# Swapping the operands of a one-hot sort product, splitting its address steps into two bfloat16 halves, and counting with the first matching steps

## The reference

```python
xn = layernorm(x)
agg = segment_sum(xn[dst] * edge_weight[:, None], src)     # rows gathered per edge, summed per source node
gnn = relu((xn + agg) @ W1 + b1) @ W2 + b2
x2 = x + gnn + head_mix(xn)                # 8 heads, k'v over all nodes, then q @ kv, plus xn
y  = x2n + sum over the top 2 of 16 experts of weight * expert(x2n)   # x2n = layernorm(x2)
out = x2 + layernorm(y) * gamma + beta
```

## Time and profile before

| | us |
|---|---|
| median of 3 runs | 2087.97 |
| lowest, highest | 2083.77, 2088.9 |
| the profiled execution, its own time | 2086.33 |
| its span | 2084.2 |
| TensorE matmul busy | 1814.0 |
| VectorE busy | 1411.1 |
| ScalarE busy | 741.2 |
| GpSimd busy | 1206.1 |

### The profile page before, as it was taken

How to read it: one execution, slowest core, us unless ns; L and a number is a source line. 1 busy time by engine, 2 the same in 40 slices (tenths; PEclk the granted TensorE clock), 3 DMA queues, 4 the chain that set the end, 5 groups by cost and what they waited for, 6 DMA issues and landing times. The chain is left out here.

```text
span 2084.2 us, 43884 instructions
## 1 busy us (share of the span) xinstructions
PE 1814.0 (87%) x12300; PEld 1634.0 (78%) x12300; DVE 1411.1 (68%) x4015; ACT 741.2 (36%) x2167; POOL 1206.1 (58%) x1244
## 2 busy tenths in 40 slices
PE   6306999758889999999999999999977999999986
PEld 4206889657878888888888888878766999999974
DVE  5899788758996777677767776657554555555547
ACT  5806778500101333333333332222222333333347
POOL 1003444477777777777777777777703555555424
PEclk9657999979999999999999999999978999999999
DMA  5000101054444444444444444444425642222248
GB/s 174 0 0 21 39 22 39 22 166 149 137 132 120 129 127 129 130 134 129 128 129 128 130 125 125 123 121 128 120 84 163 208 126 72 72 72 72 69 148 316
DMA packets 130018, 232.33 MB, mean 111 GB/s; under 512 B 25990, under 2 KB 82616, under 8 KB 129703
## 3 DMA queue, kind: packets, MB, share of 16 engines
q0 software_dynamic: 56096, 144.39, 23.8%
q1 hardware_dynamic: 46039, 59.76, 8.8%
q10 hardware_dynamic: 27696, 25.83, 3.9%
HBM read 187.46 MB, written 42.43 MB: 110 GB/s over the span
## 5 line engine op out<-in xcount | busy, mean ns | idle before, releaser
L1337 POOL DMA_INDIRECT lower<-xn_rows,lower x858 | 826.9, 964 | 261.5 <-issue 232.8
L1502 DVE TENSOR_SCALAR lower<-bank,lower 128x128 f32<-128x128 f32 x960 | 347.1, 404 | 69.6 <-issue 53.1
L1362 PE MATMUL bank<-ones,ident 128*128 128x128 f32 x2376 | 322.5, 278 | 23.3 <-DVE xh L1519 17.8
L1362 PEld LDWEIGHTS bank<-ones,ident 128*128 128x128 f32 x2376 | 307.4, 192 | 40.4 <-DVE xh L1519 20.7
L1378 PE MATMUL bank<-lower 128*128 x960 | 292.2, 386 | 19.9 <-SPq L1207 13.1
L1519 DVE TENSOR_TENSOR xh<-xh,bank 128x256 f32 x480 | 199.3, 415 | 158.4 <-PE bank L1379 156.9
L1379 PE MATMUL bank<-lower 128*128 x960 | 287.3, 380 | 0.0
L608 POOL DMA_INDIRECT edge_records_sorted<-lower x112 | 113.2, 1011 | 292.3 <-ACT lower L771 266.7
L2003 DVE TENSOR_SCALAR arena<-bank,b_tile 128x128 f32<-128x128 f32 x456 | 128.4, 345 | 166.4 <-PE bank L1881 166.4
L1881 PEld LDWEIGHTS bank<-arena 128*128 128x128 f32 x1824 | 224.6, 194 | 14.6 <-ACT arena L1936 8.9
L1881 PE MATMUL bank<-arena 128*128 128x128 f32 x1824 | 225.6, 278 | 8.1 <-ACT arena L1936 8.1
(11 more groups left out here) (347 smaller groups left out, 2594.7 us busy)
## 6 DMA issues: line engine op xcount, KB each, us to landing
lower<-xn_rows,lower POOLq DMA_INDIRECT x858
lower<-in_L_ffn_w SPq DMA_DIRECT2D x16, 512.0 KB
upper<-in_L_ffn_w SPq DMA_DIRECT2D x16, 512.0 KB
xn_rows<-xh SPq DMA_DIRECT2D x7, 896.0 KB, 4.1
lower<-xn_rows ACTq DMA_DIRECT2D x49, 128.0 KB
xn_rows<-lower ACTq DMA_DIRECT2D x49, 128.0 KB
x_plus_beta<-lower ACTq DMA_DIRECT2D x49, 128.0 KB
upper<-in_x SPq DMA_DIRECT2D x1, 6144.0 KB
```

What stands on the lines that cost most here:

```text
L1337: pool.indirect_dma_start(edge_rows[:, t % ROUND, :], None, xn_dram, bass.IndirectOffsetOnAxis(source.bitcast(U32)[:, t:t + 1], 0)).then_i ...
L1362: pe.matmul(sums_at(u)[:, 0:P], ident[:], ones[:], start=True, stop=True)
L1502: dve.tensor_scalar(edge_sel[:, (2 * u + h) % ESEL, :], iota_gather, lane[:, at:at + 1], weight_s[:, at:at + 1], ALU.is_equal, ALU.mult).t ...
```

## The change

The sort product takes `row_hot` as the stationary operand and `moving` as the moving one; its sums go from PSUM to `quads` in one ScalarE copy, and the transpose, `quads_across` and two semaphores are gone. The mask `past_m` is a bfloat16 matrix of zeros and ones, and the steps no longer multiply it on DVE: they are the moving operand `steps_b`, one column for a group, with the step's multiple of 128 on partitions 0 to 49 and its rest on partitions 64 to 113, both exact in bfloat16. DVE makes these in nine small operations before the first group. The counts stand behind distances 1 to 7. The ranks go to bank 3; a slot's `turn` waits until they have been read, instead of `second`, and `ranks` waits for the copy of the turn before it.

```diff
-        past_m = [carve(NQ * P)]
-        steps_col = carve(2 * NGRP)
+        past_m = [carve(NQ * P // 2).bitcast(BF16) for _ in range(2)]
+        LOW = 64
+        KB = LOW + NT + 1
+        first_col, step_col = carve(NGRP), carve(NGRP)
+        step_i, low_step = carve(NGRP).bitcast(I32), carve(NGRP).bitcast(I32)
+        steps_b = carve(NGRP // 2).bitcast(BF16)
...
-                if d % 4 == 3:
-                    count(d // 4)
+                if d <= NR:
+                    count(d - 1)
...
                 for c in range(NQ):
-                    mm = pe.matmul(bank[2 + p][:, c:c + 1], past_m[p][0:NT + 1, c * P:(c + 1) * P], ones[0:NT + 1, 0:1],
+                    mm = pe.matmul(bank[2 + p][:, c:c + 1], past_m[p][0:KB, c * P:(c + 1) * P], steps_b[0:KB, ds(g, 1)],
                                    start=True, stop=True)
...
                 if looped(r) or r >= 1 or i >= 2:
-                    pe.wait_ge(s_qx, g - 1)
+                    pe.wait_ge(s_qcp, g - 1)
                 for e in range(GC):
-                    mm = pe.matmul(bank[6 + p][0:NQ * QW, 0:P], moving[p][:, e].rearrange("p c w -> p (c w)"),
-                                   row_hot[p][:, e, :], start=e == 0, stop=e == GC - 1)
+                    mm = pe.matmul(bank[6 + p][:, 0:NQ * QW], row_hot[p][:, e, :], moving[p][:, e].rearrange("p c w -> p (c w)"),
+                                   start=e == 0, stop=e == GC - 1)
                 mm.then_inc(s_qmm, 1)
-                pe.wait_ge(s_qx, g + 1)
-                pe.sem_inc(s_apart, 1)
-                pe.transpose(bank[1][:, p * P:p * P + NQ * QW], quads_across,
-                             ident[0:NQ * QW, 0:NQ * QW]).then_inc(s_qT, 1)
...
                 act.wait_ge(s_qmm, 2 * g + 2)
-                act.activation(quads_across, bank[6 + p][0:NQ * QW, 0:P], ACT.Copy).then_inc(s_qx, 1)
-                act.wait_ge(s_qT, g + 1)
...
-                act.activation(quads[i], bank[1][:, p * P:p * P + NQ * QW], ACT.Copy).then_inc(s_qcp, 1)
+                act.activation(quads[i], bank[6 + p][:, 0:NQ * QW], ACT.Copy).then_inc(s_qcp, 1)
...
-            dve.tensor_copy(steps_col[0:NT + 1, :], bank[0][0:NT + 1, 0:2 * NGRP]).then_inc(s_dve, 1)
+            dve.memset(first_col, 0.0).then_inc(s_dve, 1)
+            dve.memset(steps_b, 0.0).then_inc(s_dve, 1)
+            dve.tensor_copy(step_col[high, :], bank[0][high, NGRP:2 * NGRP]).then_inc(s_dve, 1)
+            dve.tensor_copy(step_i[high, :], bank[0][high, NGRP:2 * NGRP]).then_inc(s_dve, 1)
+            dve.wait_ge(s_dve, n.add(5 + NQ))
+            dve.tensor_copy(first_col[high, :], bank[0][high, 0:NGRP]).then_inc(s_dve, 1)
+            dve.tensor_copy(first_col[low, :], bank[0][high, 0:NGRP]).then_inc(s_dve, 1)
+            dve.tensor_scalar(low_step[high, :], step_i[high, :], P - 1, None, ALU.bitwise_and).then_inc(s_dve, 1)
+            dve.wait_ge(s_dve, n.add(3))
+            dve.tensor_tensor(steps_b[high, :], step_col[high, :], low_step[high, :], ALU.subtract).then_inc(s_dve, 1)
+            dve.tensor_copy(steps_b[low, :], low_step[high, :]).then_inc(s_dve, 1)
...
-                dve.tensor_scalar(past_m[p][0:NT + 1, :], quad_number[0:NT + 1, :], steps_col[0:NT + 1, ds(g, 1)],
-                                  steps_col[0:NT + 1, ds(g + NGRP, 1)], ALU.is_ge, ALU.mult).then_inc(s_mov, 1)
+                dve.tensor_scalar(past_m[p][0:KB, :], quad_number[0:KB, :], first_col[0:KB, ds(g, 1)], None,
+                                  ALU.is_ge).then_inc(s_mov, 1)
...
-            while any(u + d - T_SECOND in turn_unit for d in (-1, 0, 1)):
+            while u in turn_unit or u - 1 in turn_unit:
                 u += 1
...
-        gate_at, ranks_at = bank[6][:, D:D + NX], bank[5][:, D:D + NX]
+        gate_at, ranks_at = bank[6][:, D:D + NX], bank[3][:, 0:NX]
```

More of the change, by code:

```diff
@@ L192, in gps_layer @@
         group_wgt = [carve(GC) for _ in range(2)]
-        past_m = [carve(NQ * P)]
-        steps_col = carve(2 * NGRP)
+        past_m = [carve(NQ * P // 2).bitcast(BF16) for _ in range(2)]
[4 more added lines that the diff above has]
+        steps_b = carve(NGRP // 2).bitcast(BF16)
         quad_idx = [carve(NQ).bitcast(U32) for _ in range(4)]
         quads = [carve(NQ * QW) for _ in range(4)]
-        quads_across = carve(P)[0:NQ * QW, :]
         aside = carve(NGRP)
@@ L316, in gps_layer @@
         past_all = xn_rows[:, 0:NJ * (NX - 1)]
-        past_m.append(xn_rows[:, 2 * F:2 * F + NQ * P])
-        assert 2 * F + NQ * P <= GT * D
         assert NJ * (NX - 1) <= GT * D
@@ L495, in gps_layer @@
         s_qmm = sem("quads_summed")
-        s_qx = sem("quads_across_copied")
-        s_qT = sem("quads_transposed")
         s_qcp = sem("quads_copied")
@@ L665, in edges_tensor @@
                     differences(d + 2)
-                if d % 4 == 3:
-                    count(d // 4)
-            assert GC // 4 == NR
+                if d <= NR:
+                    count(d - 1)
+            assert GC > NR
             pe.wait_ge(s_clear, 4)
@@ L936, in edges_vector @@
             dve.wait_ge(s_pref, 2 * len(BANKS) + 2 * NGRP)
-            dve.tensor_copy(steps_col[0:NT + 1, :], bank[0][0:NT + 1, 0:2 * NGRP]).then_inc(s_dve, 1)
-            dve.wait_ge(s_dve, n.add(2 + NQ))
+            high, low = slice(0, NT + 1), slice(LOW, KB)
+            dve.memset(first_col, 0.0).then_inc(s_dve, 1)
[9 more added lines that the diff above has]
+            dve.tensor_copy(steps_b[low, :], low_step[high, :]).then_inc(s_dve, 1)
+            dve.wait_ge(s_dve, n.add(2))
             def addresses(r, i):
@@ L1161, in gps_layer @@
         assert all(turn_unit[s] + T_CHOOSE < rank_unit[s] and turn_unit[s] + 4 <= turn_unit[s + 1] for s in range(NT - 1))
-        seconds_before = lambda u: sum(a + T_SECOND < u for a in turn_unit)
+        turns_before = lambda u: sum(a < u for a in turn_unit)
         ranks_before = lambda u: sum(a < u for a in rank_unit)
@@ L1400, in ranks @@
                         pe.wait_ge(s_hsum, s)
-                    pe.wait_ge(s_x2, seconds_before(rank_unit[s]))
+                    pe.wait_ge(s_hTe, turns_before(rank_unit[s]))
                     pe.matmul(ranks_at, ones_pb, hot_sum, start=True, stop=False)
@@ L1405, in turn @@
                 def turn(s):
+                    if ranks_before(turn_unit[s]):
+                        pe.wait_ge(s_place, ranks_before(turn_unit[s]))
                     pe.wait_ge(s_hin, s + 1)
@@ L1425, in second @@
                         pe.wait_ge(s_x2, s)
-                    if ranks_before(turn_unit[s] + T_SECOND):
-                        pe.wait_ge(s_place, ranks_before(turn_unit[s] + T_SECOND))
                     pe.matmul(bank[5][:, 0:D], ones[0:1, 0:P], gb2_row[0:1, :], start=True, stop=False)
```

## The result

The changed kernel takes 2197.7 us (median of 4 runs, 2195.8 to 2198.0), the kernel before 2088.4 beside it: a ratio of 1.0527, 95% interval 1.0508 to 1.0545, 109 us slower. The profiled execution took 2197.9 us, its span is 2195.9.

A forecast was written before the change was run, and what follows sets the result against it. TensorE's chain of product, copy, transpose and address products was taken to bound the sort. Sort stage +113.3, counts -1.0, steps +1.0, ranks 0 made +113 us, forecast 2200 us, range 2172 to 2212.

The forecast's parts named there:

- The clock: Edge sort: TensorE was taken to stay at 1.2 GHz for the whole stage with the swapped product.
- The first rival: Edge sort: 64-column streams keep TensorE at 2.4 GHz, period 6.6 us, -35 us, total 2053 us; chance 0.10.
- The sort's length: Edge sort: 28 periods of 12.46 us, last product ending at 519.4 us against 405.4, +114.0 us.
- The product: Edge sort on TensorE: 56 instructions at 214.5 ns each at 1.2 GHz, 12.0 us per product.
- the address products with the hand-over: Edge sort, each period: four bfloat16 address products 0.38 us, hand-over 0.07 us.
- the 0.4 us of each loop turn: Edge sort: each of six loop turns adds 0.4 us, as it had before the change.
- Product's end to first scatter: End of the sort: one copy of 0.25 us left, 1.1 us instead of 1.8, -0.7 us.
- Counts: Matching steps: counts behind steps 1 to 7 let the prefix products start at about 53.1 us, -1.0 us.
- Steps in two halves: Before the first sort group: nine small DVE operations replace one 0.20 us copy, +1.0 us (0.5 to 1.5).
- Ranks: Gather stage: moved ranks and new waits cost 0, bounds -0.5 and +1 us, since GpSimd's gathers pace it.
- the second rival: Edge sort: the clock comes and goes, half the groups at each pace, +40 us, total 2128 us; chance 0.04.
- DVE's wait: Edge sort before the change: DVE waits 1.3 us per group for the product, cited as showing the product limits.

The follow-up runs named there:

- Experiments 1 and 4: 1: changed kernel with 128-column sort streams, 2371.3 us against 2399.2; 4: kernel before with product operands swapped, transpose and second copy gone, 2546.6 us against 2399.2.
- experiment 2: Changed kernel with twenty float32 dummy products in front of the first sort product: 2490.3 us against 2399.2 for the kernel before.
- Experiment 6: Kernel before with only the counts moved behind the first matching steps: 2384.0 us against 2384.5, ratio 0.9992.

## Why the prediction was right, and by which terms

**The clock: right.** The choice on which the forecast hung was that the swapped product stays at 1.2 GHz, and every stretch of the sort from 162 us shows 0.50. Experiments 1 and 4 show the cause to be the swap and, in it, the streams of half length. The first rival, streams of 64 columns keep the full clock, fell: they neither raised it in the changed kernel nor held it in experiment 2, which began at 2.4 GHz. It wasn't wholly wrong, as they kept it there for two products. Its price was close: 2053 us was worked out for the full clock with the last product near 371 us, and the best version takes 2050 with its last product at 369.9, though with streams of 128 and the ranks back.

The Trainium skill, page "TensorE: Matmul & The Clock Gate", section "Why this matters for your kernels", names keeping TensorE continuously busy as the way to the full clock. In this trace that alone was not enough: TensorE is busy without a pause from 206 to 405 us at 0.50.

**The sort's length: 11 us too long.** The forecast moved the last product's end by 114.0 us, to 519.4; it moved by 104.5, to 509.9. Of this 1.6 us is the later start, so that the stage itself grew by 102.8. The product was right: 12.13 - 0.15 = 11.98 us, 213.9 ns an instruction against 214.5. The mis-sized terms are the address products with the hand-over, 0.45 us forecast and 0.15 measured (the four are some 40 ns apart at the lower clock, not 95: the 114-column rows that the forecast took as the nearest stream a hundred times as much), 28 x 0.30 = 8.4 us; and the 0.4 us of each loop turn, 2.4 us, which did not come at all: with TensorE never waiting, the turn is hidden.

**Product's end to first scatter:** 1.1 us forecast, 1.08 measured. What follows it shifted as a block, as said.

**Counts: no gain, small.** -1.0 us was forecast; the start did move, by -1.15, but the last prefix product came 0.55 us later. The forecast left the clock out of this term: the matching steps that now close the stage have no count among them, and the clock falls for the prefix products. Experiment 6 repeats it, and its other traces put the term at 0 within some 1 us either way.

**Steps in two halves:** +1.0 forecast; nine operations from 162.12 to 163.43 us, and the first row matrices +1.6 later, of which 0.55 is the counts': +1.07.

**Ranks: the term that failed.** It was set to 0 (bounds -0.5 and +1), because the gathers on GpSimd pace the stage. They do pace their own part, 1.27 us each; but TensorE's sums run behind them by 10 to 25 us and end the stage, and TensorE has so little time to spare that 17 waits, 15.2 us in all, leave 8 us at the end. Putting the ranks back takes 7 to 9 us away, on a chip with the same gather pace, and the distance from last gather to last sum goes from 18.5 back to 10.6 us. That the waits are those of line 1406 for line 1267 is read from the trace; no run took this wait alone away.

So the total came within 2.3 us by luck, because errors met: -11 us in the sort, +8 in the ranks, +1.6 in the counts. Between the profiled executions 113 us were forecast and 111.6 seen.

Two slips of the forecast change nothing here: 1.6 us over 28 groups is 45 us and not the 40 of the second rival, and DVE's wait is 29.8/19 = 1.6 us a group, not 1.3.

## What to carry to other kernels

Swapping the operands of a float32 product can leave its instruction count and pace at one clock alone and still double its time: look at how long the streams are beside their loads, and at whether the stage begins at the low clock (here even a warm start kept the full clock for two products only). If the swap is wanted for other reasons, stream columns that nobody reads: twice the work took half the time here. And where one engine paces a stage, look at how far behind it the others run at its end before a new wait on them is priced at nothing.

## What the runs showed of the hardware

- TensorE busy without a pause at 1.2 GHz from 206 to 405 us, and 104.9 of the next 105 us, never raised (loads of 128, streams of 64 float32 columns); with 128-column streams behind the same loads the clock rose within the first product.
- Which level such streams run at depends on what came before: two products at 2.4 GHz after a warm start, then 24 groups at 1.2 GHz. With dummies of 128-column streams in each group they ran at 2.4 GHz from 224 to 399 us.
- One-column bfloat16 products behind 128-column loads start some 40 ns apart at 1.2 GHz (0.15 us for four, up to the next product) and some 27 at 2.4 GHz (0.10 to 0.11 us for four); a float32 one takes two instructions, 216 ns each at 1.2 GHz.
- Three chips gave three times for the same kernel, 2087, 2385 and 2399 us. The gather stage holds nearly all of it (1089 us from first to last gather against 1372), with GpSimd behind TensorE's sums on the slower ones; why these lag is open.
